# Summing two key blocks of the exponentials on GpSimd ahead of the denominators' product, in the last stage of a two-layer decoder

## The reference, cut to what matters

```python
scores = jnp.einsum('bhqd,bhkd->bhqk', q, k) * HD ** (-0.5)
scores = jnp.where(causal, -1e9, scores)      # keys later than the query are masked
a = jax.nn.softmax(scores, axis=-1)
ctx = jnp.einsum('bhqk,bhkd->bhqd', a, v)     # HD = 32, H = 16, 256 queries, 256 keys
...
k_shared = jnp.einsum('bth,bthd->btd', indicator, k)
v_shared = jnp.einsum('bth,bthd->btd', gating_top1, v)
att = softmax(where(causal, einsum('bhqd,bkd->bhqk', q, k_shared) * hd ** -0.5, -inf))
y = jnp.einsum('bhqk,bkd->bhqd', att, v_shared)
```

## Time and profile before

| | |
|---|---|
| time, median of 3 runs | 2469.67 us (2468.76 to 2469.99) |
| the profiled execution: its own time, its span | 2451.03 us, 2448.9 us |
| TensorE (PE) matmul busy | 2185.6 us (89%), 12383 records |
| VectorE (DVE) busy | 1212.2 us (49%) |
| ScalarE (ACT) busy | 498.1 us (20%) |
| GpSimd (POOL) busy | 437.4 us (18%), 445 instructions |
| mean granted TensorE clock | 0.944 |

### The profile page before, as it was taken

The page is one execution under the profiler, slowest core; times in us unless marked ns, Lnnn a source line. Parts: engine busy times, 40 slices in busy tenths (PEclk is TensorE's granted clock), DMA queues, the critical chain, the costliest instruction groups (busy, mean ns, idle before and its releaser), DMA issues. The chain is left out here.

```text
span 2448.9 us, 30812 instructions
## 1 busy us (share of the span) xinstructions
PE 2185.6 (89%) x12383; PEld 1265.5 (52%) x12383; DVE 1212.2 (49%) x1811; ACT 498.1 (20%) x751; POOL 437.4 (18%) x445
## 2 busy tenths in 40 slices
PE   5888888867999989989999669899999999997964
PEld 3344444323444466645555346566665666664643
DVE  1456566655777752012222143445756666655354
ACT  1444444440000021111111011222222222121111
POOL 1111111113444413211111121101010110101000
PEclk9999999988999999999999879999999999998977
DMA  7000000004111047722211230101010110000000
GB/s 251 1 1 26 27 27 18 27 9 172 30 30 30 26 151 195 131 95 63 62 61 61 99 130 27 44 1 44 1 52 1 53 35 1 26 1 9 10 1 18
DMA packets 63856, 125.26 MB, mean 51 GB/s; under 512 B 12877, under 2 KB 13972, under 8 KB 63732
## 3 DMA queue, kind: packets, MB, share of 16 engines
q1 hardware_dynamic: 37492, 61.56, 7.6%
q10 hardware_dynamic: 19536, 43.26, 6.3%
q0 software_dynamic: 6704, 18.64, 2.7%
HBM read 92.18 MB, written 39.70 MB: 54 GB/s over the span
## 5 line engine op out<-in xcount | busy, mean ns | idle before, releaser
L863 PE MATMUL convB_conv<-kv,toep 128*128 128x512 f32 x640 | 277.8, 597 | 9.9 <-POOL kv L849 9.9
L1910 DVE RECIPROCAL tail_inv<-tail_ring 128x256 f32<-128x256 f32 x64 | 112.3, 1755 | 211.9 <-PE tail_ring L1566 211.9
L863 PEld LDWEIGHTS convB_conv<-kv,toep 128*128 128x128 f32 x640 | 122.6, 192 | 165.1 <-issue 156.6
L1294 PE MATMUL moe_gu_ps<-gu,moe_xT 128*128 x624 | 192.6, 462 | 2.2 <-DVE moe_xT L1357 2.2
L1294 PEld LDWEIGHTS moe_gu_ps<-gu,moe_xT 128*128 128x128 f32 x624 | 118.9, 191 | 79.3 <-issue 21.9
L849 POOL TENSOR_TENSOR kv<-vT,cT 128x512 f32 (+1 forms) x128 | 132.8, 1069 | 147.3 <-PE convB_conv L863 133.4
L888 DVE TENSOR_REDUCE vT<-prod 128x512 f32 (+1 forms) x128 | 138.2, 1080 | 16.7
L1741 POOL TENSOR_SCALAR_AFFINE_SELECT tail_expT<-tail_expT 128x1024 f32<-128x1024 f32 x64 | 70.9, 1107 | 368.8 <-ACT tail_expT L1803 368.7
L1312 PE MATMUL moe_y_ps<-down,moe_hT 128*128 (+1 forms) x234 | 110.7, 609 | 12.5 <-ACT moe_hT L1346 12.5
L1896 DVE TENSOR_TENSOR tail_allowed<-tail_scores,const_mask_bf 128x1024 f32<-128x1024 f32 x64 | 78.0, 1219 | 88.5 <-PE tail_scores L1518 87.9
L1735 POOL TENSOR_TENSOR tail_rstd_x<-tail_rstd_x,const_minus_half 128x2 f32<-128x2 f32 x32 | 22.3, 697 | 533.8 <-DVE tail_rstd_x L1868 533.8
(11 more groups left out here) (311 smaller groups left out, 3844.7 us busy)
## 6 DMA issues: line engine op xcount, KB each, us to landing
y_slots<-moe_y ACTq DMA_DIRECT2D x39, 256.0 KB, 2.0
toeplitz<-filt_pad SPq DMA_DIRECT2D x1, 8192.0 KB, 31.8
toep<-toeplitz SPq DMA_DIRECT2D x32, 256.0 KB, 2.6
gu<-in_L_ffn_gate_up_proj ACTq DMA_DIRECT2D x2, 2816.0 KB, 14.9
gu<-in_L_ffn_gate_up_proj SPq DMA_DIRECT2D x2, 2816.0 KB, 18.5
front_e<-in_ctx SPq DMA_DIRECT2D x8, 512.0 KB, 4.2
x_after<-x SPq DMA_DIRECT2D x8, 512.0 KB, 5.1
down<-in_L_ffn_down_proj ACTq DMA_DIRECT2D x2, 2048.0 KB, 18.3
```

What stands on the lines that cost most here:

```text
L863: ins = pe.matmul(conv[:, NC * p + lc, :], toep[p][:, lo:lo + P], kv[p][:, c].rearrange("p b i j -> p (b i j)"), start=c == 0, stop=c == lc)
L1294: ins = pe.matmul(gu_ps[:, s % 2, h, 0:HID], xT[:, c, :], wgu[c][:, e, h * HID:(h + 1) * HID], start=c == 0, stop=c == NC - 1)
L1910: link.after(dve.reciprocal(inv[c % 2][:], bank[:, S:2 * S]))
```

## The change

`causal` gets a second GpSimd instruction: behind its select, and a wait for it, it adds blocks 0 and 2 (later keys and earlier keys of the later queries) into a new fourth block 3 of the buffer. `weigh` waits for both, and multiplies the ones by blocks 1 and 3 in one product of 256 columns a strip, where there were one of 256 and one of 128. The products with the values stay. To make room for three buffers of four blocks, `picked` becomes a view of `allowed` (with a wait on VectorE's own last `pick` of a batch), and the constant `zeros` moves to the top of the memory.

```diff
-    c["zeros"] = st.sb("zeros", [32, P])
+    c["zeros"] = nc.alloc_sbuf_tensor_at("const_zeros", [32, P], F32, offset=nc.sbuf_top - 4 * P)
...
-        picked = st.sb("picked", [P, D])
...
+        picked = allowed[:, 0:2, :].rearrange("p g s -> p (g s)")
...
-        expT = [st.sb(f"expT{p}", [P, 3, 4, P]) for p in range(3)]
+        expT = [st.sb(f"expT{p}", [P, 4, 4, P]) for p in range(3)]
...
-                    pe.wait_ge(masked[kind], 4 * b + c + 1)
+                    pe.wait_ge(masked[kind], 2 * (4 * b + c) + 2)
...
-                    for kt, lo in ((0, S), (1, S + P)):
-                        for g in range(4):
-                            ins = pe.matmul(bank[32 * g:32 * g + 32, lo:2 * S].rearrange("p (n q) -> p n q", q=P), ones32[:],
-                                            e[:, 0:1, g] if kt else e[:, 1:3, g],
-                                            start=False, stop=kt == 1, skip_group_check=True)
+                    for g in range(4):
+                        ins = pe.matmul(bank[32 * g:32 * g + 32, S:2 * S].rearrange("p (n q) -> p n q", q=P), ones32[:],
+                                        e[:, 1:4:2, g], start=False, stop=True, skip_group_check=True)
...
-                    diagonal = exp_buf(kind, b, c)[:, 0:2].rearrange("p n g q -> p (n g) q")
+                    e = exp_buf(kind, b, c)
+                    diagonal = e[:, 0:2].rearrange("p n g q -> p (n g) q")
                     pool.affine_select(out=diagonal, in_=diagonal, compare_op=ALU.is_ge, fill=0.0, base=0,
                                        pattern=[[0, 8], [1, P]], channel_multiplier=-1).then_inc(masked[kind], 1)
+                    pool.wait_ge(masked[kind], 2 * (4 * b + c) + 1)
+                    pool.tensor_tensor(e[:, 3], e[:, 0], e[:, 2], ALU.add).then_inc(masked[kind], 1)
...
-                    act.activation(exp_buf(kind, b, c)[:].rearrange("p n g q -> p g n q"),
+                    act.activation(exp_buf(kind, b, c)[:, 0:3].rearrange("p n g q -> p g n q"),
...
                     elif t == 1:
                         ins.then_inc(v_a_ready, 1)
+                        dve.wait_ge(v_a_ready, b + 1)
```

More of the change, by code:

```diff
@@ L1942, in pick @@
                     bank = filled(key).rearrange("p (h d) -> p h d", d=HD)
-                    chosen = picked[:].rearrange("p (h d) -> p h d", d=HD)
+                    chosen = picked.rearrange("p (h d) -> p h d", d=HD)
                     of = ind[:, t, :].unsqueeze(2).to_broadcast([P, NG, HD])
@@ L1951, in pick @@
                     dst = k4[:, t, 0, :] if name == "k" else v_a[:, t, :]
-                    ins = dve.tensor_reduce(dst, picked[:].rearrange("p (h d) -> p d h", d=HD), AX_X, ALU.add)
+                    ins = dve.tensor_reduce(dst, picked.rearrange("p (h d) -> p d h", d=HD), AX_X, ALU.add)
                     if name == "k":
```

## The result

The change takes 2467.89 us (median of 15 runs, 2463.27 to 2472.22) where the kernel before takes 2471.62 (15 runs, 2468.76 to 2476.10): a ratio of 0.9980, with a 95% interval of 0.9972 to 0.9988. It is faster by 3.7 us by the medians; the ratio makes it 4.9, and its interval 3.0 to 6.9. I had forecast 8.2. The direction was right, the time lies inside the range, the size was not.

The account below looks back on a forecast made before the run. TensorE was taken to bound rounds 2 to 8. Terms 9.4 - 1.3 - 1.2 + 1.3 = 8.2 us saved: 2442.8 us profiled or, with 18.6 us carried over to the median, 2461.5 us; range 2456 to 2469 us.

Parts of the forecast that it names:

- Where time is saved: Last stage: time taken off TensorE shortens the span in rounds 2 to 8; the end rounds are followed wait by wait.
- 64 quads x 0.22: Denominators on TensorE, last stage: each quad saves 0.22 us at full clock, 14.1 us if all counted.
- Rounds 2 to 8: 43 of 48 quads pay 0.218 us each, 9.4 us gained; GpSimd's add costs nothing there.
- A3's saving: Full rounds: the one quad of eight that doesn't pay; it only widens TensorE's 0.33 us wait for a bank.
- The add's size: GpSimd's fp32 add of 128x512: 1.07 us taken, bounds 0.55 and 1.43 us.
- The wait in front: GpSimd waits for its own select before each add: 0.15 us each, from eight selects idling 1.2 us.
- Rounds 0 and 1: TensorE waits for the add before early P quads: cost 1.3 us in round 0, 1.2 us in round 1.
- near 1.9: Sign in the profile after: wait on GpSimd before P2's first weight load in round 0, in us.
- the waits cost clock: Rival: waits before P2 and P3 in rounds 0 and 1 lower the clock, 6.9 us lost, 2468.4 us; chance 0.12.
- Rounds 9 and 10: VectorE's chain of mixes starts sooner and the second's 0.24 us wait vanishes: 0.65 us gained each, 1.3 together.
- VectorE is held by the adds: Rival: GpSimd's adds hold two-input VectorE instructions 1.0 us each; half the adds make it 24 us slower; chance 0.05.
- VectorE's means rose: Listed sign that the forecast is wrong: mean times of VectorE's instructions higher after the change; no size given.

Follow-up runs that it names:

- Product alone: The change's memory layout without the add, one ones' product over blocks 1 and 2 (wrong results), against the kernel before: ratio 0.9943.
- wait alone: Kernel before, plus in rounds 0 and 1 an add on GpSimd that nobody reads but TensorE waits for: ratio 1.0028 to before.
- The filler: The change plus three matmuls of 256 columns ahead of the wait of P2 and P3 in rounds 0 and 1: ratio 0.9981 to before.
- The add on VectorE: The change with the add issued by VectorE, ahead of the mixes, instead of by GpSimd: ratio 0.9954 to the kernel before.
- layout alone: Kernel before with only the change's moved memory (fourth block, picked as a view, moved constant), old products, no add: ratio 0.9999.

## Why the prediction was right and wrong

**Where time is saved: right.** Product alone gave 10.6 to 17.3 us by its interval. That its 14.1 is the 64 quads x 0.22 of the working is luck: the same working lets about 12.4 of it count (9.4 in rounds 2 to 8, 1.3 in 9 and 10, 1.8 in 0 and 1), and the profile shows 12.8.

**Rounds 2 to 8: right.** Forecast 9.4, measured 10.7, with low-clock stretches of 1.7 us among it that moved. In rounds 4 and 5 the mark moves by 1.5 us a round, 7 of 8 quads, as said: A3's saving is not paid, and the gap before the second L1621 (L1623 before) grew from 0.33 to 0.45 us, for 0.55 forecast. L1565 with 512 records, 64 adds, no wait on POOL in a full round, all as listed.

**The add's size: too small.** 1.07 taken, 1.27 measured, inside the bounds of 0.55 to 1.43. By the working's own slope (1.4 us for 0.36) that is 0.8 us. The wait in front was 0.09, not 0.15: the 1.2 us that I divided by eight were mostly other idle time, only 0.2 of it behind L1748.

**Rounds 0 and 1: the term that failed.** Forecast 1.3 + 1.2 = 2.5 us, measured 7.0 and 6.7. The working follows each wait as a shift of start times at an unchanged pace, and so puts the clock at nothing in its sum. The runs show 7.3 us more of TensorE's work at the lower level, 3.7 us of loss by the estimate above. The rest of the term was sized about right: 7.0 less 3.7 leaves 3.3 us, and the forecast's 2.5 with the 0.8 for the slower add is 3.3. In the trace it is the 5.2 us more idle time less the 1.8 saved. (1.71 us before P2's weights was foreseen, as "near 1.9"; P0's two waits of 0.93 were taken as partly covered, without a number.) The whole sum closes: 8.2 forecast, less 3.7 for the clock, less 0.8 for the add, 2.0 more in rounds 2 to 10, makes 5.7, which is what the profile shows.

Where nothing else changes, the clock's share stands alone: in wait alone the same matmuls take 2.3 us longer. And it follows the waits. The kernels that leave TensorE idle 28.1 us or more up to the mark of round 1 have 30.0 to 32.7 us of matmuls at the lower level; those at 25.0 or less have 24.4 to 27.6. The filler, which keeps the add and its wait and only gives TensorE something to do, is among the latter with 25.9. The add on VectorE, with 26.6 us idle, lies between with 29.2.

**The rival "the waits cost clock" was the right mechanism**, and I gave it 0.12 with 6.9 us as its price, where it took 3.7. My argument against it was that P3's weight loads took 0.59 us behind 1.34 us of waiting. One wait that cost no clock says nothing of the stretch behind it: after the change P3's values took 1.51 us, in wait alone they took 0.86 and the lower level came later, in the projection. That the forecast's direction held owes something to rounds 2 to 10, which gave 12.7 for 10.7.

**Rounds 9 and 10.** Forecast 1.3, measured 2.0, but not as described. Round 10 after:

```profile
2443.43 1.76 DVE L1911 RECIPROCAL tail_inv<-tail_ring 128x256 f32<-128x256 f32 x1 [12.01 <-PE tail_ring L1565]
2446.01 1.76 DVE L1911 RECIPROCAL tail_inv<-tail_ring 128x256 f32<-128x256 f32 x1 [0.35 <-PE tail_ring L1565]
...
2450.26 1.75 DVE L1911 RECIPROCAL tail_inv<-tail_ring 128x256 f32<-128x256 f32 x1
```

The second mix waits 0.35 us, where I had its 0.24 vanish: first to last reciprocal is 6.83 us for 6.72. The gain came in round 9 (2.3 us at its mark).

**VectorE is held by the adds: no.** The norms' mean rose, before and after, by 4.5 us in all:

```profile
L1874 DVE TENSOR_SCALAR tail_x<-tail_x,tail_moments_x,tail_rstd_x 128x512 f32<-128x512 f32 x64 | 31.8, 541 | 3.5 <-POOL tail_rstd_x L1735 3.3
```

```profile
L1875 DVE TENSOR_SCALAR tail_x<-tail_x,tail_moments_x,tail_rstd_x 128x512 f32<-128x512 f32 x64 | 36.3, 610 | 3.6 <-POOL tail_rstd_x L1733 3.3
```

But it rose as much in layout alone, which has no add:

```profile
L1875 DVE TENSOR_SCALAR tail_x<-tail_x,tail_moments_x,tail_rstd_x 128x512 f32<-128x512 f32 x64 | 36.3, 612 | 3.6 <-POOL tail_rstd_x L1735 3.3
```

Of the 4.5 us, 3.9 are five norms that start beside a select, one in each full round; four others, beside adds, make 0.5. So the adds cost VectorE about 0.1 us each in four places, and it is the moved memory or the extra wait in VectorE's list that brought the rest; no run separates these two. All of it is covered: layout alone has before's time, and making the adds twice changed nothing. "VectorE's means rose", which I had listed as a sign of being wrong, was no such sign.

**The chip.** I carried 18.6 us from the profiled execution to the median without a reason. The profiles show its place, a middle stretch of the program that the change doesn't touch, before and after:

```profile
861.00:1049.00 188.00, 175.18 (x756) 120.13 (x756) 44.48 (x143) 38.10 (x69) 39.54 (x50) 0.97 0.66 161
```

```profile
865.60:1073.00 207.40, 182.28 (x758) 121.92 (x759) 44.49 (x143) 38.59 (x69) 39.49 (x50) 0.92 0.56 146
```

The same work takes 19.4 us longer, at a lower rate of transfers (146 for 161 GB/s) and a lower clock. The first and third group of experiments ran on a chip where before's median is 2473 to 2474 us and all show the long form; the second ran on one where it is 2451.28, and shows the short one, with the change and without. So it cancels in every ratio. Its cause stays open.

## What to carry to other kernels

A saving on the engine that bounds is worth its count times its distance between starts, less what a neighbour takes back; that held within the interval of 10.6 to 17.3 us. A wait put in its place can cost more than its length where that engine already idles, here about as much again as the waits' net cost: look at the granted clock of the stretch, and count the work that falls at the lower level, not the idle time. Put the new wait behind the work that doesn't need it, put the operation only where the producer has room, and give a small two-input operation to VectorE if it has time, since the length of the wait is the producer's duration.

## What the hardware showed that I had not expected

An add of 128x512 fp32 on GpSimd took 1262 to 1324 ns here, where L849 of the same shape takes 1069 in the same program. Both inputs and the output lie in one buffer here; no run separates that from other causes.

An instruction of VectorE with one tensor as input is held too, and by a select. L1875 has a median of 541 ns and a longest of 1315 after the change:

```profile
L1875 DVE TENSOR_SCALAR tail_x<-tail_x,tail_moments_x,tail_rstd_x x64: 534/541/1315, 1439.2 to 2458.5; 128x512 f32<-128x512 f32 x64
```

In layout alone the longest is 1432 ns. Two of its norms, the second of them held, and the select beside them:

```profile
1777.62 1.88 DVE L1875 TENSOR_SCALAR tail_x<-tail_x,tail_moments_x,tail_rstd_x 128x512 f32<-128x512 f32 x2
1778.13 1.09 POOL L1742 TENSOR_SCALAR_AFFINE_SELECT tail_expT<-tail_expT 128x1024 f32<-128x1024 f32 x1 [5.49 <-ACT tail_expT L1804]
```

Left open: why the add takes 0.2 us more, and what decides whether low stretches behind round 1, the turn from round 9 to round 10 above all, are there or not. One of 7 us is worth as much as the whole change (3 to 4 us).
